# Cross attention: the value products split in two around the next unit's scores, with PSUM banks of their own

## The reference

```
q = split_heads(x @ w_q)                     # x: 2 x 2048 x 640, 20 heads of 32
k, v       = split_heads(text @ w_k), split_heads(text @ w_v)        # 69 text tokens
k_ip, v_ip = split_heads(img @ w_k_ip), split_heads(img @ w_v_ip)    # 8 image tokens, with a mask by boxes
out = softmax(q k^T / sqrt(32)) v + softmax(q k_ip^T / sqrt(32) + mask) v_ip
return merge_heads(out) @ w_out + b_out + x
```

## Time and profile before

| | us |
|---|---|
| runs of the kernel | 440.38, 438.83, 437.20; median 438.83 |
| the profiled execution, its own time | 438.98 |
| its span | 437.2 |
| TensorE busy in it | 420.8 (96%) |
| VectorE busy | 346.8 (79%) |
| ScalarE, GpSimd busy | 134.0, 155.3 |

### The profile page before, as it was taken

One profiled execution on the slowest core, in us unless ns is written; L12 is line 12 of the kernel. 1 busy time (PEld: TensorE's weight loads), 2 busy tenths in 40 slices (PEclk: granted clock), 3 DMA queues, 4 the chain that ended last, 5 costly groups with the idle time before them and its releaser, 6 DMA issues.

```text
span 437.2 us, 17242 instructions
## 1 busy us (share of the span) xinstructions
PE 420.8 (96%) x7970; PEld 326.7 (75%) x7970; DVE 346.8 (79%) x457; ACT 134.0 (31%) x196; POOL 155.3 (36%) x128
## 2 busy tenths in 40 slices
PE   4999799989999999999999999999999999999996
PEld 3788678767777777777777777777777777777785
DVE  4578477759888998899888988899888988888712
ACT  4255344434223322342223332332223422222200
POOL 0238222555343632255324622265225422322200
PEclk9999999989999999999999999999999999999999
DMA  8987224212214321331124211321134111122333
GB/s 293 385 298 270 90 79 156 75 55 81 81 50 147 99 74 51 124 99 49 59 82 157 74 51 49 123 99 73 51 118 127 51 51 49 57 69 60 110 124 121
DMA packets 22391, 47.14 MB, mean 108 GB/s; under 512 B 2864, under 2 KB 2992, under 8 KB 22320
## 3 DMA queue, kind: packets, MB, share of 16 engines
q1 hardware_dynamic: 22320, 46.05, 30.7%
HBM read 35.55 MB, written 10.49 MB: 105 GB/s over the span
## 4 chain that ended last, share of the span: by engine, by line
PE 95%; DVE 2%; issue 1%; DMA 1%; ACT 0%
PE ps L604 67%; PE ps L656 13%; PE ps L637 8%; PE ps L684 5%; PE ps L690 1%; DMA stage<-in_w_q 1%; PE ps L728 1%; DVE prob_t L502 0%; PE ps L708 0%; DVE text_max L466 0%; DVE prob L472 0%; DVE wq_lo L558 0%; DVE stage L519 0%; ACT wq_hi L362 0%; PE ps L723 0%
## 5 line engine op out<-in xcount | busy, mean ns | idle before, releaser
L334 POOL TENSOR_TENSOR prob<-prob,rden 128x1104 f32<-128x1104 f32 x40 | 82.4, 2060 | 238.3 <-DVE rden L495 238.3
L604 PE MATMUL ps<-x_hi,wq_hi 128*128 128x512 f32 x200 | 84.9, 425 | 6.2 <-DVE x_lo L562 6.2
L368 ACT ACTIVATE q<-ps 128x512 f32<-128x512 f32 x40 | 23.8, 596 | 202.2 <-PE ps L604 202.2
L604 PE MATMUL ps<-o_hi,wo_hi 128*128 128x512 f32 x200 | 82.7, 414 | 0.0
L604 PE MATMUL ps<-x_lo,wq_hi 128*128 128x512 f32 x200 | 79.8, 399 | 0.0
L604 PE MATMUL ps<-x_hi,wq_lo 128*128 128x512 f32 x200 | 79.6, 398 | 0.0
L604 PE MATMUL ps<-o_lo,wo_hi 128*128 128x512 f32 x200 | 79.1, 395 | 0.0
L604 PE MATMUL ps<-o_hi,wo_lo 128*128 128x512 f32 x200 | 79.0, 395 | 0.0
L502 DVE STREAM_TRANSPOSE prob_t<-prob 128x1536 f32<-128x1536 f32 x40 | 70.8, 1769 | 0.0
L490 DVE TENSOR_REDUCE den<-prob 128x16 f32<-128x1104 f32 x40 | 51.9, 1296 | 19.0 <-ACT prob L372 19.0
L466 DVE TENSOR_REDUCE text_max<-ps 128x16 f32<-128x1104 f32 x40 | 52.2, 1304 | 17.3 <-PE ps L637 13.2
(11 more groups left out here) (55 smaller groups left out, 387.0 us busy)
## 6 DMA issues: line engine op xcount, KB each, us to landing
stage<-in_x SPq DMA_DIRECT2D x38, 256.0 KB, 3.3
res<-in_x SPq DMA_DIRECT2D x37, 256.0 KB, 2.7
out_tiles<-res SPq DMA_DIRECT2D x37, 256.0 KB, 2.1
wk_raw<-in_w_k SPq DMA_DIRECT2D x5, 512.0 KB, 7.0
wki_raw<-in_w_k_ip SPq DMA_DIRECT2D x5, 512.0 KB, 6.4
wv_raw<-in_w_v SPq DMA_DIRECT2D x5, 512.0 KB, 6.2
wvi_raw<-in_w_v_ip SPq DMA_DIRECT2D x5, 512.0 KB, 7.7
stage<-in_w_q SPq DMA_DIRECT2D x5, 320.0 KB, 6.7
```

The source lines that it names most:

```text
L334: nc.gpsimd.tensor_tensor(e[:, :, 0:TEXT], e[:, :, 0:TEXT], rden[:, par, 0, :].unsqueeze(2).to_broadcast([P, QT * HG, TEXT]), ALU.mult)
L368: nc.scalar.activation(q[:, c % 2, :], ps[:, Q_BANK, :], ACT.Copy, scale=SCALE).then_inc(q_copied, 1)
L604: return nc.tensor.matmul(ps[:, bank, :], w[:, g, P * kt:P * kt + P], m[:, b, kt, :], start=(n == 0), stop=(n == 3 * KD - 1))
```

## The change

For units 5 to 37 O goes to banks 6 and 7: row groups 0 and 1 to bank 6, 2 and 3 to bank 7, in interleaved pieces of 32 columns. Its 48 matmuls are split: 24 of row groups 0 and 2 (here called A), then the 32 matmuls of the next unit's scores, then 24 of row groups 1 and 3 (B), behind a wait for A's end. TensorE's step for c = 7 to 37 becomes A(c-1), S(c+1), B(c-1), q(c+2), out(c-6); at c = 6 q(8) stands ahead of A(5); c = 38 is the same without q. Units 0 to 4, 38 and 39 keep O in banks 0 to 3 and in one piece. At c = 5 O(4) comes behind all of q(7). ScalarE: copy_v(c-1) ahead of exp(c+1) up to c = 5; from c = 7 o_high(c-1), exp(c+1), copy_q(c+2). VectorE's order changes at c = 38 and 39 alone. The last five outputs get other banks, and out(33) goes to bank 4.

```diff
-        Q_BANK, OUT_BANK, SPARE_BANK = 4, 5, 6
-        LAST_BANKS = [Q_BANK, SPARE_BANK, OUT_BANK, 0, 1]
+        Q_BANK, OUT_BANK = 4, 5
+        LAST_BANKS = [6, 7, Q_BANK, OUT_BANK, 0]
         O_COL = 320
-        o_blocks = ps[:, 0:QB, O_COL:O_COL + QT * SQ].rearrange("p a (n r) -> p n a r", r=SQ)
+        o_apart = ps[:, 0:QB, O_COL:O_COL + QT * SQ].rearrange("p a (n r) -> p n a r", r=SQ)
+        O_BANK = 6
+        o_pair = ps[:, O_BANK:O_BANK + 2, 0:2 * QT * SQ]
+        o_joined = o_pair.rearrange("p b (n s r) -> p n b (s r)", s=2, r=SQ)
...
+        def is_apart(c):
+            return c < KD or c >= UNITS - AHEAD_Q
...
+        def out_bank(c):
+            return Q_BANK if c == UNITS - BEHIND_OUT - 1 else OUT_BANK
...
                     if c > 0:
                         copy_v_part(c - 1)
                         copy_vt(c - 1)
+                        copy_v(c - 1)
                     exp(c + AHEAD_S)
-                    if c > 0:
-                        copy_v(c - 1)
                     copy_q(c + AHEAD_Q)
...
-                elif exists(c + AHEAD_Q):
+                elif c == KD + 1:
                     copy_q(c + AHEAD_Q)
                     o_high(c - 1)
                     exp(c + AHEAD_S)
                 else:
+                    o_high(c - 1)
                     if exists(c + AHEAD_S):
                         exp(c + AHEAD_S)
-                    o_high(c - 1)
+                    if exists(c + AHEAD_Q):
+                        copy_q(c + AHEAD_Q)
...
             def step(c):
-                late = c >= UNITS - AHEAD_Q
                 if exists(c + AHEAD_S):
                     shift_text(c + AHEAD_S)
                     shift_img(c + AHEAD_S)
-                if late:
+                if c == UNITS - 1:
                     finish(c - BEHIND_OUT)
-                if c == UNITS - 1:
+                turn(c)
+                if c <= KD or c == UNITS - AHEAD_Q:
+                    sums(c + AHEAD_S)
+                if c == UNITS - AHEAD_Q:
+                    finish(c - BEHIND_OUT)
+                if exists(c - 1):
                     o_low(c - 1)
-                turn(c)
-                if (late or c <= KD) and exists(c + AHEAD_S):
+                if KD < c < UNITS - AHEAD_Q:
                     sums(c + AHEAD_S)
-                if exists(c - 1) and c < UNITS - 1:
-                    o_low(c - 1)
-                if exists(c + AHEAD_S) and not late and c > KD:
-                    sums(c + AHEAD_S)
-                if exists(c - BEHIND_OUT) and not late:
                     finish(c - BEHIND_OUT)
...
+            def value(c, kb, a, j):
+                b, t, g = place(c)
+                rows = slice(SQ * a, SQ * a + SQ)
+                p_t = prob_t[rows, c % 2, :, SQ * kb:SQ * kb + SQ].rearrange("p (n h) r -> p n h r", h=HG)
+                if is_apart(c):
+                    dst = ps[DH * j:DH * j + DH, a, O_COL:O_COL + QT * SQ]
+                else:
+                    dst = ps[DH * j:DH * j + DH, O_BANK + a // 2, 0:2 * QT * SQ].rearrange(
+                        "p (n s r) -> p n s r", s=2, r=SQ)[:, :, a % 2, :]
+                return nc.tensor.matmul(dst, v[rows, KB * b + kb, P * g + DH * j:P * g + DH * j + DH], p_t[:, :, j, :],
+                                        start=(kb == 0), stop=(kb == KB - 1))
...
-                if c >= 3:
+                if 3 <= c <= KD + 2:
                     pe.wait_ge(o_lo_done, c - 2)
...
+            def make_o_and_scores(c, s):
+                values_ready(c)
+                for kb in range(KB):
+                    for a in (0, 2):
+                        for j in range(HG):
+                            last = value(c, kb, a, j)
+                last.then_inc(o_half_made, 1)
+                make_scores(s)
+                pe.wait_ge(o_half_made, c - KD + 1)
+                for kb in range(KB):
+                    for a in (1, 3):
+                        for j in range(HG):
+                            last = value(c, kb, a, j)
                 last.then_inc(o_made, 1)
...
-                    if c < KD:
-                        make_q(c + AHEAD_Q, whole[9:15])
-                        make_o(c - 1)
-                    else:
-                        make_q(c + AHEAD_Q, whole[9:12])
-                        make_o(c - 1)
-                        make_q(c + AHEAD_Q, whole[12:15])
+                    make_q(c + AHEAD_Q, whole[9:15])
+                    make_o(c - 1)
...
             def late_step(c):
 
                 if exists(c + AHEAD_S):
-                    make_scores(c + AHEAD_S)
-                make_out(c - BEHIND_OUT)
-                make_o(c - 1)
-                if c == UNITS - 1:
+                    make_o_and_scores(c - 1, c + AHEAD_S)
+                    make_out(c - BEHIND_OUT)
+                else:
+                    make_out(c - BEHIND_OUT)
+                    make_o(c - 1)
                     make_out(c - BEHIND_OUT + 1)
                     make_o(c)
...
                 else:
-                    make_scores(c + AHEAD_S)
-                    make_q(c + AHEAD_Q, whole)
-                    make_o(c - 1)
-                    if exists(c - BEHIND_OUT):
-                        make_out(c - BEHIND_OUT)
+                    if c == KD + 1:
+                        make_q(c + AHEAD_Q, whole)
+                    make_o_and_scores(c - 1, c + AHEAD_S)
+                    if c > KD + 1:
+                        make_q(c + AHEAD_Q, whole)
+                    make_out(c - BEHIND_OUT)
```

More of the change, by code:

```diff
@@ L164, in xattn_kernel @@
         o_made = sem("o_made")
+        o_half_made = sem("o_half_made")
         o_hi_done = sem("o_hi_done")
@@ L505, in o_low, with finish @@
             def o_low(c):
-                b, t, g = place(c)
                 dve.wait_ge(o_hi_done, c + 1)
[L508 to L512, removed]
+                src, dst = o_views(c, o_lo)
+                _, hi = o_views(c, o_hi)
+                nc.vector.tensor_tensor(dst, src, hi.bitcast(F32), ALU.subtract).then_inc(o_lo_done, 1)
+            def finish(c, bank=None):
                 tile, loaded, n = out_tile(c)
@@ L518, in finish @@
                     dve.wait_ge(bias_loaded, 16)
+                if bank is None:
+                    bank = out_bank(c)
                 nc.vector.scalar_tensor_tensor(out=tile, in0=ps[:, bank, :],
@@ L621, in make_q, with score, scores_ready @@
                         last.then_inc(q_made, 1)
-            def make_scores(c):
+            def score(c, n, j, half):
                 b, t, g = place(c)
+                rows = slice(DH * j, DH * j + DH)
+                at = P // 2 * half
+                return nc.tensor.matmul(ps[at:at + P // 2, j, TOKENS * n:TOKENS * n + TOKENS],
+                                        q[rows, c % 2, P * n + at:P * n + at + P // 2], k[rows, b, g, :], start=True, stop=True)
+            def value(c, kb, a, j):
+                b, t, g = place(c)
+                rows = slice(SQ * a, SQ * a + SQ)
+                p_t = prob_t[rows, c % 2, :, SQ * kb:SQ * kb + SQ].rearrange("p (n h) r -> p n h r", h=HG)
+                if is_apart(c):
+                    dst = ps[DH * j:DH * j + DH, a, O_COL:O_COL + QT * SQ]
[4 more added lines that the diff above has]
+                                        start=(kb == 0), stop=(kb == KB - 1))
+            def scores_ready(c):
                 pe.wait_ge(q_copied, c + 1)
@@ L631, in make_scores, with values_ready @@
                     pe.wait_ge(scores_used, c)
[L632 to L643, removed]
+            def values_ready(c):
                 pe.wait_ge(turned, c + 1)
@@ L646, in make_o, with make_scores @@
                     pe.wait_ge(v_copied, c + 1)
+                if c >= 1:
+                    pe.wait_ge(o_lo_done, c)
+            def make_scores(c):
+                scores_ready(c)
+                for n in range(QT):
+                    for j in range(HG):
+                        for half in range(2):
+                            last = score(c, n, j, half)
+                last.then_inc(scores_made, 1)
+            def make_o(c):
+                values_ready(c)
                 if exists(c + 2):
                     pe.wait_ge(scores_used, c + 3)
-                if c >= 1:
-                    pe.wait_ge(o_lo_done, c)
                 for kb in range(KB):
                     for a in range(QB):
-                        rows = slice(SQ * a, SQ * a + SQ)
-                        p_t = prob_t[rows, c % 2, :, SQ * kb:SQ * kb + SQ].rearrange("p (n h) r -> p n h r", h=HG)
                         for j in range(HG):
-                            last = nc.tensor.matmul(ps[DH * j:DH * j + DH, a, O_COL:O_COL + QT * SQ],
-                                                    v[rows, KB * b + kb, P * g + DH * j:P * g + DH * j + DH], p_t[:, :, j, :],
-                                                    start=(kb == 0), stop=(kb == KB - 1))
+                            last = value(c, kb, a, j)
```

(16 more changed lines are left out.)

9 lines of the change are left out of this document (6 added, 3 removed).

## The result

| | us |
|---|---|
| the changed kernel, median of 4 runs | 451.53 (448.88 to 454.57) |
| the kernel before, 4 runs on the same chip | 439.61 (437.20 to 441.04) |
| ratio, 95% interval | 1.0257 [1.0212, 1.0302] |
| the profiled execution, its own time | 448.88, its span 447.1 |

The change makes the kernel 2.6% slower, between 2.1% and 3.0%. The forecast was 438.6, in a range up to 444.0: the prediction was wrong.

What follows compares the result with a forecast made beforehand. TensorE alone was taken to bound the kernel. From 438.98: -3.97 (early stalls) - 1.65 (clock) + 0.6 + 0.5 (new waits) + 4.3 (33 longer steps) = 438.8, forecast 438.6 against the median; range 427.5 to 444.

Steps and rivals of the forecast that it cites:

- The sum for a step: TensorE's step A, S, B, q, out: 9.79 us against 9.66, over 33 steps +4.3 us.
- The clock: Half-clock stretch at 91.2 to 94.5 us goes with the wait, saving 1.65 us; the pause at 45.3 to 47.7 stays.
- Two places without that cover: TensorE waits for VectorE once at A(6), 0.6 us, and once at c = 39 for o_low(37), 0.5 us.
- Early steps: TensorE's stalls at O(2), O(3), O(4) and S(7), 3.97 us, all go; exp is late next, with thin margin.
- No drain: Rival, chance 0.22: changes between small shapes A, S, B are free, 10.6 us less in 33 steps, so 428.0.
- The halves are slow: Rival, chance 0.12: each pass of A and B might show its weight load, a half takes 0.80 us, so 447.2.
- The early gain lost: Rival, chance 0.08: wait moves to o_low or clock falls after the 45 us pause; 3 to 5 us lost, 442.5.
- The middle claim: Whole kernel within 1% of no change, chance 0.58: early steps give 5.6 us, the 33 others take nearly all back.

Runs made afterwards that it cites:

- e1: The changed kernel with 12 extra value matmuls (48 instructions) ahead of O(4): 445.79 us, ratio 1.0100 to the kernel before.
- e2: The changed kernel with 58 extra value matmuls (232 instructions) ahead of O(4): 458.09 us, ratio 1.0393 to the kernel before.
- e6: e5 with 51 extra value matmuls (204 instructions) ahead of O(4): 457.74 us, ratio 1.0404 to the kernel before.
- e10: e9 with 51 extra value matmuls (204 instructions) ahead of O(4): 437.35 us, ratio 0.9931 to the kernel before.
- e5: The changed kernel with q(c+2) as first block of every step from 6 to 37, then A, S, B, out: 441.96 us, ratio 1.0026.
- e8: e3 with its last steps reordered, plus 24 extra value matmuls (96 instructions) ahead of O(0): 443.76 us, ratio 1.0090 to the kernel before.
- e3: The kernel before with the early edits alone, step order q, S, out, O, no halves or new banks: 438.37 us, ratio 0.9944.
- e9: e3 with its last steps reordered and VectorE's step 37 as finish(31), turn(37), o_low(36), sums(38): 434.36 us, ratio 0.9861 to the kernel before.

## Why the prediction was wrong

- **The sum for a step** failed, by what it left out. Its terms were right: drains 0.20 and 0.15 (0.20 and 0.16 forecast), a half 0.66 to 0.67 (0.67), the step 9.73 (9.79). But it priced A, S and B one by one and took for granted that 320 small instructions in a row reach TensorE in time. e1, e2, e6 and e10 show that they don't when a piece of the stream ends late in the group: 7.6 us in stops and 3.1 at half clock, in the profiled execution. Without them and the 0.7 at A(6) it would have been near 437.5, and e5 measures that case: ratio 1.0026, with a wait and a half-clock stretch of its own at the end.
- The trace of before had the hint. Its pause inside S(3) was set aside in **The clock** as something that "stays"; e8 shows that it is of the same kind. A pause inside a group of one shape, with no wait in it, deserved the question of what the engine lacked, and whether the change would make such groups longer.
- **Two places without that cover**: A(6) waited 1.3 us, not 0.6. The step counted the transpose and not o_low(5) behind it (0.65 us), though `values_ready` names both. The wait at c = 39 was 0.2 where 0.5 was forecast: O(38) starts at 419.54, 0.51 after out's last product at 419.03, where 0.32 is the change of shape. o_low(37) ended at 419.39 and not near 419.9.
- **Early steps** were right: O(2), O(3), O(4) and S(7) wait no more, and exp's delay brought no new wait. e3 has this gain without the halves.
- **The clock**: the half-clock stretch at 91 us went, but others came, behind the stops and the wait at A(6). That a new pause brings a half-clock stretch with it stood only in a rival.
- **The rivals**: "No drain" fell with the drains. "The halves are slow" fell: six passes a tile in 0.66 us show no weight load, and no run shows the refill pause of 0.09 that its sum took. The Trainium skill's rule ("TensorE: Matmul & The Clock Gate", The mechanism) that weight loads overlap matmuls in flight only where the row group differs, from which the prediction argued for this rival, isn't borne out by this row. Its side, slower than before, was the right one, by another mechanism. "The early gain lost" was not what happened.
- The middle claim, that the halves themselves are worth nothing here, holds: 9.73 against 9.65 before, and 9.61 in e3 and e9, which keep O whole. They bring two drains between small shapes, and these cost more than the order of the blocks saves.

**What stays open.** Why the packet is later in some steps than in others, so that the stops of the change are 0.9 to 1.6 us in steps 31 to 37, 0.5 in step 17 and 0.2 in 27, and missing in step 29, where a piece ends within a few passes of the same place. The queue that brings instructions shows one packet in the changed kernel between 314.9 and 315.3 us, ahead of A's start at 315.39; for step 31 its packet lies between 336.0 and 336.5, an us after A's start at 334.92:

```profile
q8 instruction: 1, 0.02, 18.3%
...
q8 instruction: 1, 0.02, 11.7%
```

So in one case the packet came earlier, in terms of the work, than in the other, and the stops follow it. What sets the moment at which it starts no run here tells. A packet takes 0.9 to 1.9 us in this profile, and whether other DMA traffic stretches it was not tested. Nor is it shown why only some stops are followed by half clock: the one of 1.64 us in step 31 is, those of 1.08, 0.91 and 1.25 after it aren't.

## What to carry to other kernels

Small fp32 matmuls use up TensorE's instructions at some 130 a microsecond, and a row of them longer than one piece of the stream (about 256 instructions) can outrun the supply; put a block of long products between such groups, and don't merge them to save a change of shape without pricing this. Test a kernel of this kind by adding some instructions early in the program: if its time moves by more than their work, its speed is luck of the grid. And when a wait is priced, go through every condition of it, each with what stands behind it on its engine.

## What was not expected of the hardware

- A piece of TensorE's stream is about 127 matmul passes and as many weight loads here, 16.5 KB by the queue's row, laid out from the start of the program. This agrees with the Trainium skill ("Runtime: NRT & Kernel Launch", Instruction fetch mechanics), which has 16 KiB blocks of 256 instructions fetched in order.
- The same section calls the cost of crossing a block's end mostly hidden. With long products between small groups of up to 192 instructions it is: e9 has no stop of over 0.15 us after 50 us. In the group of 320 small instructions it isn't: stops of 0.5 to 1.8 us in the changed kernel, up to 1.9 in e6. Nor is it at the first long products behind that group: 0.7 to 0.8 us in e2's steps 29, 31 and 33. In step 31 of the changed kernel the packet starts at 336.40, over 2 us before TensorE goes on at 338.74, while 128 passes at the pace of B's (0.67 us for 48) take 1.8 us.
- Adding instructions that do nothing useful can make a kernel 1.5% faster (e1 against the change, ratios 1.0100 and 1.0257) or 3.6% slower (e6 against e5, 457.74 and 441.96).
